# A graph network and mixture-of-experts kernel: part of the edge-range search moved from ahead of the block loop into it

## What is computed

```python
col = dst                                            # sorted
xn = layernorm(x)
out1 = segment_sum(edge_attr, col, n)
cnt  = segment_sum(ones, col, n)
out2 = where(cnt > 0, segment_max(edge_attr, col, n), 0)
out3 = out1 / maximum(cnt, 1)
h = concatenate([xn, out1, out2, out3, u[0] repeated], axis=1)
x = x + (relu(h @ W1 + b1) @ W2 + b2 + xn)           # hidden 1024
# then layernorm(x), a router over 16 experts, the two best of them per node,
# each relu(x @ w1[e] + b1[e]) @ w2[e] + b2[e], weighed by softmax,
# a residual and a layernorm, and x added again
```

## Time and profile before

| | |
|---|---|
| median of 3 runs | 1259.35 us (1257.04 to 1261.62) |
| the profiled execution | 1254.82 us, its span 1252.9 us |
| granted clock over the span | 0.93 |
| PE busy (matmul) | 1088.9 us, 87% |
| DVE, POOL, ACT busy | 838.2, 804.0, 650.1 us |
| DMA | 282.73 MB, mean 226 GB/s |

### The profile page before, as it was taken

The page is one execution under the profiler, slowest core; times in us unless marked ns, Lnnn a source line. Parts: engine busy times, 40 slices in busy tenths (PEclk is TensorE's granted clock), DMA queues, the critical chain, the costliest instruction groups (busy, mean ns, idle before and its releaser), DMA issues.

```text
span 1252.9 us, 26862 instructions
## 1 busy us (share of the span) xinstructions
PE 1088.9 (87%) x6460; PEld 949.9 (76%) x6461; DVE 838.2 (67%) x3164; ACT 650.1 (52%) x1974; POOL 804.0 (64%) x1030
## 2 busy tenths in 40 slices
PE   2002999999999999999999998889999999999935
PEld 1002888888888888888888888879999999999911
DVE  4989999799979979992577801476322222247788
ACT  5864565666566656656655524222233232345554
POOL 4786666666676666666866335556666666656686
PEclk7555999999999999999999999899999999999965
DMA  9995758777686867459411047765666666688855
GB/s 318 278 309 168 288 206 308 272 279 271 224 301 230 311 250 257 178 215 320 147 40 46 26 164 256 263 224 197 208 214 207 216 208 211 215 290 295 278 180 157
DMA packets 131330, 282.73 MB, mean 226 GB/s; under 512 B 25900, under 2 KB 38576, under 8 KB 131114
## 3 DMA queue, kind: packets, MB, share of 16 engines
q1 hardware_dynamic: 94230, 218.41, 49.9%
q0 software_dynamic: 26048, 43.47, 11.3%
q10 hardware_dynamic: 10964, 19.96, 4.5%
HBM read 167.27 MB, written 114.25 MB: 225 GB/s over the span
## 4 chain that ended last, share of the span: by engine, by line
PE 40%; POOL 29%; issue 17%; DVE 4%; ACT 4%; DMA 4%; POOLq 1%; SPq 0%; DVEq 0%; ACTq 0%
PE ps L1327 16%; PE ps L1335 15%; POOL mem L636 12%; DMA mem<-in_dst_dram,mem 2%; POOL mem L698 2%; POOL mem L681 2%; POOL mem L700 2%; PE ps L1216 2%; PE ps L1313 2%; PE ps L1202 2%; PE ps L1204 2%; ACT mem L852 2%; POOL mem L623 1%; POOL mem L689 1%; POOL mem L674 1%
## 5 line engine op out<-in xcount | busy, mean ns | idle before, releaser
L1054 ACT ACTIVATE mem<-ps,mem 128x128 f32<-128x128 f32 x452 | 129.3, 368 | 284.3 <-PE ps L1327 283.5
L1327 PEld LDWEIGHTS ps<-mem 128*128 128x128 f32 x1808 | 219.9, 193 | 19.3 <-issue 12.7
L1327 PE MATMUL ps<-mem 128*128 128x128 f32 x1808 | 223.8, 278 | 10.9 <-issue 10.4
L1335 PE MATMUL ps<-mem 128*128 x904 | 214.7, 381 | 0.8 <-issue 0.7
L1424 DVE TENSOR_TENSOR_SCAN mem<-ps,mem 128x80 f32<-128x80 f32 x960 | 208.0, 316 | 0.3
L1202 PE MATMUL ps<-mem 128*128 128x250 f32 x800 | 205.4, 379 | 3.1 <-ACT mem L952 1.7
L1428 DVE TENSOR_TENSOR_SCAN mem<-ps,mem 128x80 f32<-128x80 f32 x960 | 208.0, 342 | 0.0
L1204 PE MATMUL ps<-mem 128*128 128x250 f32 x800 | 202.2, 375 | 0.0
L1216 PE MATMUL ps<-mem 128*125 128x256 f32 x800 | 181.6, 380 | 0.7 <-ACT mem L952 0.7
L1335 PEld LDWEIGHTS ps<-mem 128*128 128x128 f32 x904 | 163.6, 191 | 19.2 <-issue 1.3
L1202 PEld LDWEIGHTS ps<-mem 128*128 128x128 f32 x800 | 151.2, 192 | 21.0 <-ACT mem L952 2.6
(11 more groups left out here) (282 smaller groups left out, 1712.9 us busy)
## 6 DMA issues: line engine op xcount, KB each, us to landing
mem<-in_L_ffn_w_dram SPq DMA_DIRECT2D x129, 512.0 KB, 9.8
run_sum<-mem SPq DMA_DIRECT2D x80, 480.0 KB, 5.5
run_max<-mem SPq DMA_DIRECT2D x80, 480.0 KB
mem<-in_edge_attr_dram SPq DMA_DIRECT2D x72, 480.0 KB
mem<-expert_rows SPq DMA_DIRECT2D x26, 256.0 KB, 5.3
x_rows<-mem ACTq DMA_DIRECT2D x25, 256.0 KB, 3.8
x_normed<-mem ACTq DMA_DIRECT2D x25, 256.0 KB, 2.8
mem<-in_x_dram ACTq DMA_DIRECT2D x24, 256.0 KB
```

What stands on the lines that cost most here:

```text
L1054: ins = act.activation(hT[b][:, c, :], bank(2 + b, c * P, (c + 1) * P), ACT.Relu, bias=eb1c[:, bass.ds(e, 1), c])
L1327: ins = pe.matmul(bank(2 + b, f * P, (f + 1) * P), w1now[q][:, c, f * P:(f + 1) * P], XgT[b][:, c, :], start=(c == 0), stop=(c == DC - 1))
L1335: ins = pe.matmul(bank(6 + b, 0, D), hT[b][:, c, :], w(c * D, D), start=(c == 0), stop=(c == FC - 1))
```

## The change

The 50 tiles are now three sets: `FIRST_TILES` 30 to 49, `LATER_TILES` 20 to 29 and `LAST_TILES` 0 to 19.

- Ahead of the loop GpSimd issues seeks for tiles 25 to 49 (five groups), then does the index math of tiles 30 to 49 itself up to the edge counts (24 small operations in place of VectorE's, on GpSimd a multiply and an add where VectorE had one fused operation), with the two copies of starts as DMAs of its own queue, tells VectorE (`starts_ready`), seeks tiles 20 to 24, and goes on to `gather(0)`.
- VectorE does the edge counts and reciprocals of tiles 30 to 49 between its first and second chunk, and the whole index math of tiles 20 to 29 behind the second. SP copies the starts for those alone.
- ScalarE finds all row numbers ahead of the loop as before, but counts only six groups there, the sixth behind the moments of block 0.
- The 20 seeks of tiles 0 to 19 stand at the end of GpSimd's `rows_step(i)` in blocks 0 to 6, three a block (`SEEKS`), two in block 6. They have six buffers of their own. ScalarE counts them in `gnn_step(i)` of the same block, right ahead of `take_g(i)`.
- The index math of tiles 0 to 19 is done by GpSimd in pieces at the ends of blocks 7 to 12, a power of −1 in place of VectorE's reciprocal.

```diff
-    LATE = TILES - 4 * ST
+    FIRST_TILES, LATER_TILES = slice(TILES - 4 * ST, TILES), slice(TILES - 6 * ST, TILES - 4 * ST)
+    LAST_TILES = slice(0, TILES - 6 * ST)
+    SEEKS = 3
+    SOUGHT = LAST_TILES.stop // SEEKS
+    EARLY_GATHERS = 5
...
+        def start_edges(e, op, c):
+            op(e.tensor_scalar(startn[:, c], rowf[:, c], float(ROWE), 0.5 * ROWE, ALU.mult, ALU.add))
+            op(e.tensor_scalar(tA[:, c], rows_seen[:, c], 0.5, None, ALU.mult))
+            op(e.tensor_tensor(startn[:, c], startn[:, c], tA[:, c], ALU.add))
...
+            def seek_late(j):
+                n = 2 * SEEKS
+                if j == 0:
+                    pool.wait_ge(rows_ready, GROUPS)
+                if j >= n:
+                    pool.wait_ge(late_counted, j - n + 1)
+                pool.indirect_dma_start(out=SRL[:, j % n, :], out_offset=None, in_=dst2,
+                                        in_offset=bass.IndirectOffsetOnAxis(rowU[:, j:j + 1], 0)).then_inc(late_got[j % n], 16)
...
+            def end_edges(c):
+                pool.dma_start(nextn[0:NT - 1, c], startn[1:NT, c]).then_inc(pool_ends, 16)
+                pool.dma_start(nextn[NT - 1:NT, c], startn[0:1, c.start + 2:c.stop + 2]).then_inc(pool_ends, 16)
+
+            def search_later(i):
+                c = LAST_TILES
+                if i <= SOUGHT:
+                    for j in range(SEEKS * i, min(SEEKS * (i + 1), c.stop)):
+                        seek_late(j)
+                elif i == SOUGHT + 1:
+                    pool.wait_ge(late_counted, c.stop)
+                    start_edges(pool, op, c)
+                    end_edges(c)
+                elif i == SOUGHT + 2:
+                    start_pieces(pool, op, c)
+                elif i == SOUGHT + 3:
+                    start_rows(pool, op, c)
+                elif i == SOUGHT + 4:
+                    next_pieces(pool, op, c)
+                elif i == SOUGHT + 5:
+                    pool.wait_ge(pool_ends, 64)
+                    edge_counts(pool, op, c)
+                elif i == SOUGHT + 6:
+                    op(pool.tensor_tensor(tB[:, c], tA[:, c], minus_one, ALU.pow))
+                    op(pool.tensor_tensor(rch[:, c], tB[:, c], has[:, c], ALU.mult))
+
+            for n in range(EARLY_GATHERS):
+                seek(n)
+            pool.wait_ge(row_counted, TILES - FIRST_TILES.start)
+            start_edges(pool, op, FIRST_TILES)
+            end_edges(FIRST_TILES)
+            start_pieces(pool, op, FIRST_TILES)
+            start_rows(pool, op, FIRST_TILES)
+            next_pieces(pool, op, FIRST_TILES)
+            pool.sem_inc(starts_ready, 1)
+            seek(EARLY_GATHERS)
...
                 if i + 2 < MACROS:
                     by_level(i + 2, behind_cut)
                 else:
                     behind_cut(0)
+                search_later(i)
...
+            def count_late(i, g, b, seeks=SEEKS):
+                for a in range(seeks):
+                    j = SEEKS * i + a
+                    act.wait_ge(late_got[SEEKS * b + a], (g + 1) * 16)
+                    if not isinstance(j, int) or j:
+                        act.wait_ge(late_counted, j)
+                    act.activation(late_junk, SRL[:, SEEKS * b + a, :], ACT.Sign, bias=below[:, bass.ds(j, 1)], scale=-1.0,
+                                   accum_out=rows_seen[:, bass.ds(j, 1)]).then_inc(late_counted, 1)
...
                     take_x2(i - 1)
+                if seeks:
+                    count_late(i, g, b, seeks)
                 take_g(i, g, b)
...
+            dve.wait_ge(starts_ready, 1)
+            dve.wait_ge(pool_ends, 32)
+            edge_counts(dve, op, FIRST_TILES)
+            reciprocals(FIRST_TILES)
+            dve.sem_inc(index_ready, 1)
             edges(1, 0, 1)
```

More of the change, by code:

```diff
@@ L228, in gnn_moe_kernel @@
         rpow = k.take(2, parts=NT)
+        minus_one = k.take(LAST_TILES.stop, parts=NT)
         slot_no = k.take(SLOT_TILES)
@@ L288, in gnn_moe_kernel @@
         CR = [a.take(2, EF) for _ in range(2)]
+        SRL = a.take(2 * SEEKS, ROWE, parts=NT, dt=I32)
+        late_junk = a.take(ROWE, parts=NT)
         a = Area(mem, WORK + 12 * D, WORK_END)
@@ L374, in gnn_moe_kernel @@
         row_counted = sem("row_counted")
+        late_got = [sem(f"late_row_got{i}") for i in range(2 * SEEKS)]
+        late_counted, index_step = sem("late_row_counted"), sem("index_step")
+        pool_ends = sem("pool_ends_got")
         starts_ready, ends_got, index_ready = sem("starts_ready"), sem("ends_got"), sem("index_ready")
@@ new lines, in start_pieces, with start_rows @@
+        def start_pieces(e, op, c):
+            op(e.tensor_copy(endn[:, c.start:c.stop:2], startn[:, c.start + 1:c.stop:2]))
+            op(e.tensor_scalar(tA[:, c], startn[:, c], float(E - 1), None, ALU.min))
+            floors(e, op, tB[:, c], tA[:, c], T, 0)
+        def start_rows(e, op, c):
+            floors(e, op, tC[:, c], tB[:, c], P, PAD)
+            op(e.tensor_scalar(gatei[:, c.start // 2:c.stop // 2], tC[0:1, c.start:c.stop:2], -1.0, float(CHUNKS), ALU.mult, ALU.add))
+            op(e.tensor_scalar(tC[:, c], tC[:, c], -2.0 * P * T, None, ALU.mult))
+            op(e.tensor_tensor(tA[:, c], tA[:, c], tC[:, c], ALU.add))
+            op(e.tensor_scalar(IX[:, c, 0], tA[:, c], float(T * (PAD + FULL * P)), None, ALU.add))
@@ new lines, in next_pieces @@
+        def next_pieces(e, op, c):
+            op(e.tensor_scalar(tB[:, c], tB[:, c], 1.0, None, ALU.add))
+            op(e.tensor_scalar(cp[:, c], tB[:, c], float(T), None, ALU.mult))
+            op(e.tensor_scalar(tB[:, c], tB[:, c], float(PIECES - 1), None, ALU.min))
+            floors(e, op, tC[:, c], tB[:, c], P, PAD)
+            op(e.tensor_scalar(tC[:, c], tC[:, c], -2.0 * P, None, ALU.mult))
+            op(e.tensor_tensor(tB[:, c], tB[:, c], tC[:, c], ALU.add))
+            op(e.tensor_scalar(IX[:, c, 1], tB[:, c], float(PAD + FULL * P), None, ALU.add))
@@ new lines, in edge_counts @@
+        def edge_counts(e, op, c):
+            op(e.tensor_copy(endn[:, c.start + 1:c.stop:2], nextn[:, c.start:c.stop:2]))
+            op(e.tensor_tensor(cp[:, c], endn[:, c], cp[:, c], ALU.subtract))
+            op(e.tensor_scalar(cp[:, c], cp[:, c], 0.0, 1.0, ALU.max, ALU.min))
+            op(e.tensor_tensor(tA[:, c], endn[:, c], startn[:, c], ALU.subtract))
+            op(e.tensor_scalar(has[:, c], tA[:, c], 1.0, None, ALU.min))
+            op(e.tensor_scalar(tA[:, c], tA[:, c], 1.0, None, ALU.max))
@@ L468, in edge_chunk @@
                 sp.dma_start(carry[bass.ds(s * P, P)], CR[b].rearrange("p s f -> p (s f)")).then_inc(st_car[b], 16)
[L469 to L473, removed]
+                if isinstance(s, int) and s == 1:
+                    c = LATER_TILES
+                    sp.wait_ge(starts_ready, 2)
+                    sp.dma_start(nextn[0:NT - 1, c], startn[1:NT, c]).then_inc(ends_got, 16)
+                    sp.dma_start(nextn[NT - 1:NT, c], startn[0:1, c.start + 2:c.stop + 2]).then_inc(ends_got, 16)
                 sp.wait_ge(st_sum, (s + 2) * 16 * len(CUTS))
@@ L587, in _ @@
             st.mark(pool.memset(epsc, EPS))
+            st.mark(pool.memset(startn[:, TILES:TILES + 2], float(E)))
+            st.mark(pool.memset(minus_one, -1.0))
             st.mark(pool.memset(rpow, -0.5))
@@ L613, in _, with seek @@
             pool.tensor_scalar(below, node, 0.5, None, ALU.subtract).then_inc(below_ready, 1)
-            for n in range(GROUPS):
+            def seek(n):
                 lo, hi = TILES - (n + 1) * ST, TILES - n * ST
@@ new lines, in _, with op @@
+            ix = Steps(pool, index_step)
+            def op(ins):
+                ix.mark(ins)
+                ix.wait()
+            def end_edges(c):
[22 more added lines that the diff above has]
+                    op(pool.tensor_tensor(rch[:, c], tB[:, c], has[:, c], ALU.mult))
@@ L721, in rows_step @@
                     norm1(i + 1)
-                if i + 2 == (TILES - LATE) // 2:
+                if i + 2 == (TILES - FIRST_TILES.start) // 2:
                     pool.wait_ge(index_ready, 2)
@@ L889, in _ @@
                 pick_rows(n)
-                count_row(n - 2)
-            for n in range(GROUPS - 2, GROUPS):
-                count_row(n)
+                if n - 2 < EARLY_GATHERS:
+                    count_row(n - 2)
+            def count_late(i, g, b, seeks=SEEKS):
[6 more added lines that the diff above has]
+                                   accum_out=rows_seen[:, bass.ds(j, 1)]).then_inc(late_counted, 1)
             def carry_in(i, g, b):
@@ L1003, in take_g, with gnn_step @@
                 ins.then_inc(g_out, 1)
-            def gnn_step(i, g, b, to=None):
+            def gnn_step(i, g, b, to=None, seeks=0):
                 more = not isinstance(i, int) or i + 1 < MACROS
@@ L1042, in _ @@
             take_turned(0, 0, 0)
-            gnn_step(0, 0, 0)
-            gnn_step(1, 0, 1)
```

(22 more changed lines are left out.)

13 lines of the change are left out of this document (6 added, 7 removed).

## The result

The changed kernel takes 1282.63 us (median of 4 runs, 1280.61 to 1285.39), the kernel before in the same runs 1258.38. The ratio is 1.0188, 95% interval 1.0164 to 1.0212: 1.9% slower, and 0.4 us from the forecast of 1283. The profiled execution has a span of 1280.6 us against 1252.9.

A forecast was written before the change was run, and what follows sets the result against it. GpSimd's queue was taken to bound the head, PE the loop. Head −14.4, ring +36.3 and index math +1.6 gave +23.5 on the profiled 1254.8, 1278.3; with 4.5 us to the timed median, about 1283, range 1262 to 1299.

The forecast's parts named there:

- The head: Ahead of the loop: only 30 of 50 seeks stay, so block 0's gathers start earlier; 14.4 us saved (12.8 to 16.4).
- The landing: Block 0's gathers, beside the third edge chunk's load: 7.3 us to land (bounds 5.3 and 8.9).
- the next wait: Block 0's gathers wait for chunk 0, in DRAM at 79.31, after GpSimd's queue ends at 75.3; start near 79.5 us.
- The ring: Blocks 0 to 6: add_rows, six gathers, three seeks, landing, count, take_g, add_rows; 30.0 us against 24.42, 36.3 us lost in all.
- Index math: GpSimd in blocks 7 to 12: mostly hidden in 3.8 us idle, blocks 7 and 12 late; 1.6 us (0 to 3).
- The sum: Whole kernel: −14.4 + 36.3 + 1.6 = +23.5 us, forecast 1283.
- (a): Loop: the seeks hide, PE and not the count holds take_g; 1246.5 us; chance 0.14 with its milder form.
- only GpSimd's issues count: Milder form of (a), loop: landing not on the way, 1.2 us a block, net −7, 1252 us; within (a)'s 0.14.
- (b): PE's clock, loop: pauses bring back 1.2 GHz, block 32 us, +12 us in 6 blocks, 1295; chance 0.10.
- (c): Head: GpSimd's small operations take 1 us each, gathers start at 88, head gives 6 us; 1291; chance 0.06.

The follow-up runs named there:

- the profile without the seeks: The changed kernel without the 20 seeks in the loop and without their counts (wrong ranges for tiles 0 to 19): ratio 0.9879 to the kernel before.
- the count one block later: The changed kernel with block i counting the seeks of block i - 1 and the index math one block later: ratio 0.9933 to the kernel before.
- the kernel with filled pauses: The changed kernel with 12 more matmuls, results never read, between layer 1's halves in blocks 1 to 6: ratio 1.0168 to the kernel before.

## Why the prediction was right

**The head.** Forecast 14.4 us saved (12.8 to 16.4), measured 16.9, just over the upper end. The landing was sized right (7.3 forecast, 7.9 measured). The start was not: chunk 0 was in DRAM at 75.87, 3.3 us after its carry store was issued, where the trace of before had 6.5. So it wasn't the next wait after all; GpSimd's own queue was, with its first gather at 76.48 against my 75.3 for its end. Why the store landed faster was not tested; in the kernel before SP issued two small copies right behind it, which the change gave to GpSimd. The two plain DMAs cost 0.66 and 0.56 us, not 1.5 each; three operations were longer (1.56, 0.76 and 0.78 us between 62 and 65.4 us) and made up for it.

**The ring.** This is the step that decided, and it is shown: opening it alone is worth 32 us. Its terms against the block at 165.77: the last seek is issued 24.04 us after add_rows, forecast 24.06. From there to the next add_rows it took 6.2 us, forecast 4.6 + 1.35 = 5.95. The landing median in the loop was 4.7 (3.4 to 7.7), forecast 4.6 from the earlier trace rows:

```profile
L684 POOL DMA_INDIRECT mem<-in_dst_dram,mem x20: 1210/1214/1216, 126.3 to 311.9; - x20
...
DMA to landing us min/median/max: 3.4/4.7/7.7
```

Block 0 lost 5.0 us (forecast 4.6), taken as its add_rows, 11.84 us earlier than before, against the 16.85 of the head. Blocks 1 to 5 lost 30.6 (28.0) and block 6 lost 5.0 (4.1): 40.6 in all against 36.3 forecast. The term that was small is what follows the landing. I had put one count on the ring; when the seeks land together, as in the block shown, all three are on it, at 0.68 each. In the block at 134.94 (30.8 us) the third landing and one count came last, as forecast. The 17 us less (19 instead of 36) that the estimate by the Trainium skill (DMA: Bandwidth & Descriptors, "Anatomy of one DMA — SWDGE (gpsimd) path") would have given didn't come: no seek landed in under 3.4 us.

**Index math.** Forecast 1.6 us, measured 0.4. The 0.5 us forecast for block 7 were not there: GpSimd was through at 341.16 (340.60 + 0.56) and waited 1.7 us for take_g, which waited for layer 2. Block 7 is 0.4 us longer than before all the same (25.26 us, 24.87 before), and so is block 8 by 0.5; there PE set the pace, and why was not tested. Block 12 takes 24.85 against 24.41, 0.4 more. The power over 125x20 took 3.58 us, between the two ends, and fitted nearly:

```profile
340.60 0.56 POOL L695 DMA_DIRECT2D mem<-mem  x1
...
342.16 0.66 ACT L1112 ACTIVATE mem<-ps 125x256 f32<-125x256 f32 x2 [2.87 <-PE ps L1332]
...
342.89 1.30 POOL L782 TENSOR_TENSOR mem<-mem 125x512 f32<-125x512 f32 x1 [1.73 <-ACT mem L1112]
...
461.92 3.58 POOL L716 TENSOR_TENSOR mem<-mem 125x20 f32<-125x20 f32 x1
465.57 0.23 POOL L717 TENSOR_TENSOR mem<-mem 125x20 f32<-125x20 f32 x1
465.88 1.28 POOL L782 TENSOR_TENSOR mem<-mem 125x512 f32<-125x512 f32 x1
```

**The sum** came out right partly by cancelling: the head gave 2.5 us more than forecast, the ring took 4.3 more, blocks 7, 8 and 12 took 1.3 where the index math was to take 1.6. That is −16.9 + 40.6 + 1.3 = +25.0, with +24.9 at the add_rows of block 12, of which later blocks gave 0.6 back: +24.3 at the 20th and +24.3 between the medians. The spans of the two profiled executions differ by 27.7. Of the rest, 1.6 us lie between the 22nd and 23rd add_rows (33.3 us, 31.7 before) and 1.7 behind the loop. The 33.3 is also in the profile without the seeks and not in that with the count one block later, so it can't be put down to the seeks. That the measured time lies only 0.4 us from 1283 is therefore in part luck.

**The rivals.** (a), that the seeks hide: false in both forms; but "only GpSimd's issues count" describes the kernel with the count one block later, 1249.6 us where 1252 was worked out. (b), the clock: its premise is true and its price isn't. The granted clock falls to 0.89 to 0.94 in blocks 1 to 6, behind pauses of 1.85 to 4.01 us, and layer 2 ended 26.1 us after add_rows in the block shown, where (b) had 31.2; in a block whose length is set elsewhere no gain from removing the half clock could be measured. The Trainium skill (TensorE: Matmul & The Clock Gate, "HAM oscillation — how this bites in real kernels") tells of a kernel in which each wait of about 3 to 5 us brought half rate back; the trace agrees and shows it behind a pause of 1.85 us as well. (c), slow small operations: three of 24 were slow, the others followed each other within 0.29 to 0.36 us.

## What to carry to other kernels

Work moved into an engine's idle time must fit that idle time, and a wait added for it must not lie ahead of anything that its own issuer waits for: write down the ring (who issues, what lands, who counts, whom the issuer waits for next) and add it up. A result that is needed only later should be taken one step later than it is asked for; here one index, i − 1 for i, was worth 32 us. And where a wait ends with the last of several landings, size it from the upper part of their spread, not from its median: here 3.4 to 7.7 us with a median of 4.7.

## What the runs showed of the hardware

Beyond what was expected: a power on GpSimd costs 0.73 us for 125x2 and 3.58 us for 125x20, so about 0.16 us for each further column ((3.58 − 0.73)/18), where a plain operation of 125x20 takes 0.21 to 0.31 us. A plain DMA issued by GpSimd holds it for 0.6 us, against 1.21 us and a gap of 0.30 for an indirect one of 125 rows. PE's pauses for the relu in blocks 1 to 6, of 1.85 to 4.01 us, were each followed by matmuls at the 1.2 GHz level (2.03 us for four in five of the six blocks, 1.64 in the sixth); with the pause filled, such a block had a granted clock of 1.00. The length of a pause alone doesn't tell: in the kernel with filled pauses four matmuls behind a pause of 2.99 us took 1.11 us.

The three slow operations of GpSimd in the head ran beside three operations of VectorE and ended 0.12 us or so after them:

```profile
62.04 1.48 DVE L1516 TENSOR_TENSOR mem<-mem 64x1279 f32<-64x1279 f32 x1
...
62.09 1.56 POOL L462 TENSOR_SCALAR mem<-mem 125x20 uint32<-125x20 f32 x1
...
63.56 0.82 DVE L1517 TENSOR_SCALAR mem<-mem 32x1280 f32<-32x1280 f32 x1
...
63.74 0.76 POOL L465 TENSOR_SCALAR mem<-mem 125x20 f32<-125x20 f32 x1
...
64.41 0.82 DVE L1518 TENSOR_SCALAR mem<-mem 32x1280 f32<-32x1280 f32 x1
...
64.58 0.78 POOL L466 TENSOR_SCALAR mem<-mem 125x20 f32<-125x20 f32 x1
```

In all seven kernels with these operations three of them were slow (1.34 to 1.56, then 0.73 to 0.80 and 0.76 to 0.80 us). Which ones differed from kernel to kernel, but they always lay beside the same three operations of VectorE, while beside VectorE's scans they took 0.21 to 0.28 us. So it is VectorE's operation and not GpSimd's that goes with the delay; no experiment moved it to show the cause.
